# Relative attentions: unweighed probabilities are turned, and the inverse row sums are spread by a small matmul and multiplied in where the heads are copied

## The chip, the core and the metric

The kernel runs on one core of a Trainium2 chip. Its time is the device time of one execution in microseconds (us). Before the change it is 2825.42 us, the median of 3 runs (2820.93 to 2825.87).

The engines are named as in the profile: PE is TensorE (PEld its weight load, which overlaps the matmuls), DVE is VectorE, ACT is ScalarE, POOL is GpSimd, SP issues the DMAs (SPq is its queue).

## The reference, cut to what matters

The program is a chain of eight layers on a tensor of 4 x 512 tokens with 128 features. Two of them are attentions with 16 heads of 8 features, in which the distance of query and key also has its own learned key and value. The first is causal, the second sees all keys. Each head of each query has one row of 512 scores, and a softmax over it:

```python
# first relative attention (causal); rk, rv = embk[rel], embv[rel]
att = jnp.einsum('bhtd,bhsd->bhts', q, k) * scale + jnp.einsum('bhtd,tsd->bhts', q, rk)
att = jnp.where(causal[None, None], att, -jnp.inf)
att = jax.nn.softmax(att, axis=-1)
y = jnp.einsum('bhts,bhsd->bhtd', att, v) + jnp.einsum('bhts,tsd->bhtd', att, rv)
# second relative attention (all keys), same shape of work
attn = jax.nn.softmax((score1 + s2) / scaling, axis=-1)
w1 = jnp.einsum('bhqk,bhkd->bhqd', attn, vh)      # with the values v = h @ Wv.T + bv
w2 = jnp.einsum('qnk,qkd->qnd', se, rel_v)         # with the values of the distance
out = (w1 + w2) ...
```

A softmax row is exp(score - max) divided by its sum. Both products behind it are linear in the row, so the division may stand before them or behind them.

## The kernel before, in words

Each relative attention is one `core` step. It goes over 256 tiles. A tile is 8 queries by 16 heads of one lane (one of the 4 sequences): its 128 rows lie on the 128 partitions, and its columns are the keys, up to 512. 16 tiles are a batch (one block of 128 queries of a lane), so that there are 16 batches in each attention. All engines walk through the same steps `T_` = 0, 2, 4, ..., two tiles in each, and each stage handles the tile `T_ - lag`: scores at lag 6 (`SCORES`), turning at 8, the distance values at 10, their choice at 12. Each engine's code is written in the order in which it executes, and semaphores join the engines; there is no scheduler. The order within a step of two tiles is:

- PE: `scores` of two tiles (5 matmuls each of 128 rows in fp32r, one more in the causal attention), every other step `spread` (2 matmuls into bank 6), `turn` of the two tiles of the step before (up to 4 transposes each, L1033), `embedded` (small strip matmuls with the distance values), a part of `values` in steps 24, 26, 28 and 30 of a batch (mod 16: 8, 10, 12, 14), and `fold` at the steps in `FOLDS`.
- DVE: `chosen` twice (L1694), the copies of the position part (L1724, L1729, second attention only) and of the heads (L1745 in the first, L1747 in the second attention), `maxima` twice (L1709), then `normal` of the first tile (a reciprocal at L1686, a product over the whole row at L1687), every other step `diagonal` (L1702), and `normal` of the second tile.
- ACT: `exps` twice (L1364, with the row's sum as a second output), then the copies of the two turned tiles out of PSUM (by L1271).
- POOL: spreads queries with a mask (L1899, L1909) some steps ahead, and the values of a lane once per lane.

PE's `turn` waits for `r_normal`, the two rows weighed by DVE. PE's 4th matmul of the scores waits for `r_diagonal` when a new group of four tiles begins. `scores` of tile t + 2 waits for the exponentials of tile t, since there are two banks for scores. `values` accumulate a batch's heads in bank 7, and DVE copies them to `centered`.

## Time and profile before

| what | value |
|---|---|
| median of 3 runs | 2825.42 us (2820.93 to 2825.87) |
| the profiled execution | 2822.93 us, its span 2821.2 us |
| PE busy over the span | 2640.0 us (94%) |
| DVE, ACT, POOL busy | 1943.3, 1858.7, 1051.2 us |
| mean granted clock of TensorE | 0.977 of full speed |
| first relative attention, first to last matmul of its tiles | from about 616 to 1060 us |
| second relative attention | from about 1153 to 1719 us |

The profile shows one execution. "Busy" is the time in which an engine has an instruction in flight; for PE the ends of matmuls are modelled, and since matmuls overlap in the pipeline, their mean duration is longer than the distance from one to the next. That distance is read from the start times. A wait of PEld is partly covered by a matmul that still runs; a wait of PE itself is not covered, but begins only after the modelled end of the last matmul. The true stall lies between the two.

### The profile page before, as it was taken

How to read it: one execution, taken by the hardware profiler on the slowest of the kernel's cores; microseconds unless marked ns; L12 is line 12 of the kernel's file. 1: busy time of each engine (PE TensorE's matmuls, PEld its weight loads, DVE VectorE, ACT ScalarE, POOL GpSimd, SP SyncE). 2: the span in 40 equal slices, each digit the busy share in tenths (PEclk: the TensorE clock that was granted, in tenths of full speed). 3: DMA queues.
4: the chain of work that ended last, by engine and by line, in shares of the span. 5: the costliest groups of instructions: out<-in, count | busy, mean ns of one | idle time of the engine just before them, and what ended most of it. 6: DMA issues, size and time to landing. Idle time of an engine off the chain costs nothing.

```text
span 2821.2 us, 62773 instructions
## 1 busy us (share of the span) xinstructions
PE 2640.0 (94%) x23748; PEld 1795.2 (64%) x23748; DVE 1943.3 (69%) x5617; ACT 1858.7 (66%) x4392; POOL 1051.2 (37%) x876
## 2 busy tenths in 40 slices
PE   7999999899999998999999997999898997989998
PEld 5665657458888884688888884554455563553554
DVE  5564747488878777789898986774774326765774
ACT  5676767427676671678777875885776416866874
POOL 2322324113333320555555552552453014542551
PEclk9999999999999999999999999999999999999999
DMA  1010000000000001000000003210210002201210
GB/s 56 1 43 1 13 9 1 4 10 2 2 2 2 2 2 56 24 2 2 2 2 2 2 2 114 50 42 8 65 46 12 24 1 72 50 24 34 50 39 16
DMA packets 35278, 63.09 MB, mean 22 GB/s; under 512 B 11526, under 2 KB 15654, under 8 KB 33830
## 3 DMA queue, kind: packets, MB, share of 16 engines
q1 hardware_dynamic: 34982, 59.07, 7.6%
q8 instruction: 195, 3.19, 0.5%
q14 instruction: 101, 0.83, 0.1%
HBM read 23.48 MB, written 1.15 MB: 9 GB/s over the span
## 4 chain that ended last, share of the span: by engine, by line
PE 73%; DVE 12%; ACT 7%; issue 3%; SPq 2%; POOL 1%; DMA 1%; DVEq 0%; ACTq 0%; POOLq 0%
PE bank L804 63%; PE bank L1033 5%; PE bank L1153 3%; SPq L770 2%; PE bank L880 1%; ACT low L1364 1%; DVE low L1709 1%; DVE low L1687 1%; ACT work L1400 1%; ACT work L1303 1%; DVE halves L1702 1%; DMA work<-work 1%; DVE work L1589 1%; ACT bank L1279 1%; ACT squared L1281 1%
## 5 line engine op out<-in xcount | busy, mean ns | idle before, releaser
L1271 ACT ACTIVATE low<-bank 128x512 f32<-128x512 f32 (+3 forms) x512 | 427.7, 945 | 0.0
L804 PE MATMUL bank<-table_keys,halves 128*128 128x512 f32 (+3 forms) x1536 | 417.9, 380 | 1.2 <-ACT low L1364 1.0
L1364 ACT ACTIVATE low<-bank,low 128x512 f32<-128x512 f32 (+23 forms) x384 | 227.2, 592 | 248.9 <-DVE low L1709 244.9
L804 PE MATMUL bank<-work 128*64 128x128 f32 (+6 forms) x4192 | 344.9, 296 | 41.4 <-DVE work L1796 20.4
L804 PEld LDWEIGHTS bank<-work 128*64 128x64 f32 (+4 forms) x4192 | 249.7, 145 | 205.3 <-issue 151.7
L1709 DVE TENSOR_REDUCE low<-bank 128x1 f32<-128x512 f32 (+22 forms) x512 | 286.3, 569 | 94.5 <-PE bank L804 89.9
L1899 POOL TENSOR_TENSOR halves<-squared,const 128x512 fp32r<-128x512 f32 x128 | 136.9, 1070 | 510.9 <-PE bank L804 510.9
L1271 ACT ACTIVATE work<-bank 128x512 f32<-128x512 f32 (+4 forms) x389 | 199.8, 539 | 136.0 <-PE bank L804 70.2
L804 PEld LDWEIGHTS bank<-table_keys,halves 128*128 128x128 f32 x1536 | 243.6, 190 | 47.8 <-issue 13.3
L1400 ACT ACTIVATE work<-work 128x192 f32<-128x192 f32 (+1 forms) x512 | 218.8, 431 | 37.7 <-DVE work L1789 37.7
L1948 POOL TENSOR_TENSOR work<-work 128x768 f32<-128x768 f32 x128 | 187.7, 1466 | 136.0 <-DVE work L1800 136.0
L1953 POOL TENSOR_TENSOR work<-work 128x512 f32<-128x512 f32 x128 | 163.6, 1278 | 180.8 <-DMA work<-work 167.6
L1687 DVE TENSOR_SCALAR low<-low 128x512 f32<-128x512 f32 (+23 forms) x384 | 214.0, 557 | 13.5
L804 PE MATMUL bank<-halves 128*128 128x128 f32 (+27 forms) x1024 | 206.0, 283 | 11.5 <-DVE halves L1702 11.3
L804 PEld LDWEIGHTS bank<-halves 128*128 128x128 f32 x1024 | 181.5, 189 | 51.3 <-DVE halves L1702 23.9
L804 PE MATMUL bank<-normed,slot 128*128 128x512 f32 x440 | 198.8, 594 | 6.2 <-ACT work L1322 2.4
L804 PE MATMUL bank<-work,slot 128*128 128x512 f32 (+1 forms) x408 | 194.4, 614 | 5.6 <-ACT work L1271 5.6
L1275 ACT ACTIVATE squared<-centered 128x512 f32<-128x512 f32 x80 | 50.0, 629 | 222.1 <-DVE centered L1520 221.8
L1033 PE MATMUL bank<-const,low 128*128 128x128 f32 x1248 | 180.3, 274 | 5.0 <-ACT low L1271 3.9
L1857 POOL TENSOR_SCALAR normed<-normed,slot 128x512 f32<-128x512 f32 x48 | 75.4, 1571 | 286.8 <-DVE normed L1527 286.5
L804 PE MATMUL bank<-centered,const 128*128 128x512 f32 x256 | 145.0, 649 | 25.4 <-ACT centered L1377 25.4
L1942 POOL TENSOR_TENSOR work<-work 128x512 f32<-128x512 f32 (+1 forms) x64 | 107.5, 1680 | 150.7 <-DVE work L1603 149.5
(202 smaller groups left out, 5701.5 us busy)
## 6 DMA issues: line engine op xcount, KB each, us to landing
work<-work SPq DMA_DIRECT2D x512, 64.0 KB, 2.0
slot<-in_wW SPq DMA_DIRECT2D x4, 1605.5 KB, 7.0
slot<-in_wA SPq DMA_DIRECT2D x4, 837.0 KB, 6.2
table_low<-embv_padded SPq DMA_DIRECT2D x2, 1536.0 KB, 6.3
table<-in_dft SPq DMA_DIRECT2D x1, 3072.0 KB, 11.9
slot<-in_wE SPq DMA_DIRECT2D x2, 584.0 KB, 4.3
const<-in_const SPq DMA_DIRECT2D x1, 1094.5 KB, 5.3
squared<-in_x SPq DMA_DIRECT2D x4, 256.0 KB, 6.3
```

The lines of the kernel that those rows point to most:

```text
L804: return pe.matmul(o, l, r, start=start, stop=stop)
L1033: last = pe.transpose(o[:, b * P:(b + 1) * P], PR[t.G % 4][:, b * P:(b + 1) * P], ident)
L1153: last = pe.transpose(o[:, (2 * a + blk) * P:(2 * a + blk + 1) * P], PW[:, s.n % 3, 2 * u + a, blk * P:(blk + 1) * P], ident)
L1271: return act.activation(dst, src, ACT.Identity)
L1364: act.activation(PR[t.G % 4][:, 0:n], bank[t.G % 2][:, 0:n], ACT.Exp, bias=NBR[:, t.G % 4:t.G % 4 + 1], accum_out=RSR[:, t.G % 8:t.G % 8 + ...
L1400: last = act.activation(row, row, ACT.Exp, scale=-1.0, bias=small[:, one:one + 1], accum_out=small[:, 4 + one:5 + one])
L1687: dve.tensor_scalar(row, row, inverse, None, ALU.mult).then_inc(sem("r_normal"), 1)
L1709: dve.tensor_reduce(out=NBR[:, t.G % 4:t.G % 4 + 1], in_=bank[t.G % 2][:, 0:score_columns(t)], axis=AX.X, op=ALU.max, negate=True).then_in ...
L1899: pool.tensor_tensor(A4[:, half, Q % 2, :].rearrange("p (t h) -> p t h", h=HEADS_R), bc(one_lane.unsqueeze(2), [P, 4 * QG, HEADS_R]), bc(k ...
L1942: pool.tensor_tensor(row, row, bc(small_a[:, 8 + s.i % 4, 0:LOC].unsqueeze(2), [P, LOC, 256 - lo]), ALU.mult)\
L1948: pool.tensor_tensor(row, row, bc(small_w[:, s.n % 4, 8:12].unsqueeze(2), [P, 4, 192]), ALU.mult).then_inc(sem("w_weighed"), 1)
L1953: pool.tensor_tensor(R1[:, s.n % 3, :], R1[:, s.n % 3, :], R2[:, s.n % 3, :], ALU.add).then_inc(sem("w_added"), 1)
```

## The change

1. `normal` is gone on DVE (a reciprocal and a product over the row for each of 512 tiles). The exponentials stay unweighed: `turn` waits for `r_exp` instead of `r_normal`.
2. ACT's sums of a batch go to one array `RSR` of 16 columns (two of them in turns).
3. Once per batch, at step 22, DVE's `inverse` takes the reciprocal of 128 x 16 sums and multiplies it with a mask into `SPREAD_INVERSE` (128 x 128). PE's `inverse`, between `turn` and `embedded`, multiplies that with `head_rows` into columns 128 to 255 of bank 7, and in the second attention also with `swapped_rows` into the next 128. ACT's `inverse` copies the result to `INVERSE_SUMS` after the turned tiles. `values` of that batch (step 24) waits for that copy.
4. The copy of a batch's heads becomes a product with `INVERSE_SUMS` (first attention), and in the second a product and an addition instead of one instruction. The position copies become products. The value bias is added to two columns (`EVC`) before the second attention.
5. `FOLDS` of the second attention: the fold of a batch's first half moves from step 18 to step 24, its position copy from step 20 to 26.
6. The exact constants (568 columns) leave `const`, which becomes 1885 columns wide instead of 2189, and have a DMA of their own into `shifted`, ahead of the inputs on SP's queue.

```diff
-FOLDS, VALUES = ((24, 26), (18, 26)), 24
+FOLDS, VALUES, INVERSE = ((24, 26), (24, 26)), 24, 22
...
             sp.dma_start(const[:, :], ins["const"]).then_inc(sem("const_loaded"), 16)
+            sp.dma_start(exact_staged, ins["exact"]).then_inc(sem("exact_loaded"), 16)
...
                 def turn(t):
-                    pe.wait_ge(sem("r_normal"), t.at + 1)
+                    pe.wait_ge(sem("r_exp"), t.at + 1)
...
+                def inverse(T_):                                     # PE
+                    k = batch_after(T_, INVERSE)
+                    if k is None:
+                        return
+                    pe.wait_ge(sem("r_inverse_spread"), BATCHES * s.which + k + 1)
+                    reached(pe, "r_head_copied", BATCHES * s.which + k)
+                    last = mm(bank[7][:, P:2 * P], k_("head_rows"), SPREAD_INVERSE)
+                    if s.which:
+                        last = mm(bank[7][:, 2 * P:3 * P], k_("swapped_rows"), SPREAD_INVERSE)
+                    last.then_inc(sem("r_inverse"), 1)
...
                     if part == 0:
                         pe.wait_ge(sem("r_values_spread"), 4 * (C * s.which + lane) + 4)
-                        reached(pe, "r_head_copied", BATCHES * s.which + k)
+                        pe.wait_ge(sem("r_inverse_copied"), BATCHES * s.which + k + 1)
...
+                def inverse(T_):                                     # ACT, behind turned
...
+                    act.wait_ge(sem("r_inverse"), BATCHES * s.which + k + 1)
+                    reached(act, "r_head_copied", BATCHES * s.which + k)
+                    copy(INVERSE_SUMS[:, 0:1 + s.which, :], bank[7][:, P:(2 + s.which) * P].rearrange("p (a t) -> p a t", a=1 + s.which))\
+                        .then_inc(sem("r_inverse_copied"), 1)
...
+                        link(dve.tensor_tensor(EVC[:, 0:2], EVC[:, 0:2], bc(wt(s, WR, "bv"), [P, 2]), ALU.add))
...
-                def normal(t):
-                    inverse = RIR[:, t.G % 8:t.G % 8 + 1]
-                    row = PR[t.G % 4][:, 0:score_columns(t)]
-                    dve.wait_ge(sem("r_exp"), t.at + 1)
-                    link(dve.reciprocal(inverse, RSR[:, t.G % 8:t.G % 8 + 1]))
-                    dve.tensor_scalar(row, row, inverse, None, ALU.mult).then_inc(sem("r_normal"), 1)
+                def inverse(T_):                                     # DVE
...
+                    dve.wait_ge(sem("r_exp"), s.which * TILES + BATCH * (k + 1))
+                    reached(dve, "r_inverse", BATCHES * s.which + k)
+                    link(dve.reciprocal(RIR, RSR[:, k % 2, :]))
+                    wide = [P, BATCH, QG]
+                    dve.tensor_tensor(SPREAD_INVERSE.rearrange("p (t q) -> p t q", q=QG), bc(RIR.unsqueeze(2), wide),
+                                      bc(k_("row_query").unsqueeze(1), wide), ALU.mult).then_inc(sem("r_inverse_spread"), 1)
...
-                            copied = dve.tensor_copy(PH[rows_, one, :], bank[6][32 * one:32 * one + 32, 0:64])
+                            dve.tensor_tensor(PH[rows_, one, :], bank[6][own, 0:64], INVERSE_SUMS[own, 1, 64 * half:64 * half + 64], ALU.mult)\
...
-                            last = dve.tensor_copy(dst, o)
+                            last = dve.tensor_tensor(dst, o, weigh, ALU.mult)
...
-                            last = dve.scalar_tensor_tensor(out=dst, in0=o, scalar=wt(s, WR, "bv"), in1=dst, op0=ALU.add, op1=ALU.add)
+                            link(dve.tensor_tensor(weighed, o, weigh, ALU.mult))
+                            last = dve.tensor_tensor(dst, dst, weighed, ALU.add)
...
                     position_copy(T_)
                     head_copy(T_)
+                    inverse(T_)
                     st(maxima, SCORES)
                     st(maxima, SCORES - 1)
-                    st(normal, SCORES)
                     st(diagonal, SCORES - 2)
-                    st(normal, SCORES - 1)
```

How the instructions stand now is shown at three places. Names in them: `slot` and `low` hold DVE's results and the rows of probabilities, `halves` the spread queries, `table_keys` the keys, `bank` is PSUM; the semaphores in brackets are what a row waits for.

DVE in the second attention, steps 36 and 38 (20 and 22 of the second batch), before: the position copy, the maxima, the weighing of two rows with `diagonal` between, and the next two maxima.

```order
L1724 COPY low<-bank 32x64 [waits r_folded]
L1724 COPY low<-bank 32x64 x3
L1729 SCALAR_TENSOR_TENSOR centered<-low,centered 32x4x64 [waits r_position_copied]
L1709 TENSOR_REDUCE low<-bank 128x1 [waits r_scores,r_position_added]
L1709 TENSOR_REDUCE low<-bank 128x1 [waits r_scores]
L1686 RECIPROCAL low<-low 128x1 [waits r_exp]
L1687 TENSOR_SCALAR low<-low 128x512 [waits vector_chain]
L1702 TENSOR_TENSOR halves<-bank,const 128x512 [waits r_repeated]
L1686 RECIPROCAL low<-low 128x1 [waits r_exp]
L1687 TENSOR_SCALAR slot<-slot,low 128x512 [waits vector_chain]
L1694 TENSOR_TENSOR slot<-bank,const 128x16x8 [waits r_embedded] x2
L1709 TENSOR_REDUCE low<-bank 128x1 [waits r_scores] x2
```

The same steps now:

```order
L1724 TENSOR_TENSOR slot<-bank,const 128x16x8 [waits r_folded,r_embedded]
L1724 TENSOR_TENSOR slot<-bank,const 128x16x8 [waits r_embedded]
L1739 TENSOR_REDUCE low<-bank 128x1 [waits r_scores] x2
L1732 TENSOR_TENSOR halves<-bank,const 128x512 [waits r_repeated]
L1724 TENSOR_TENSOR slot<-bank,const 128x16x8 [waits r_embedded] x2
L1714 RECIPROCAL low<-low 128x16 [waits r_inverse,r_exp]
L1716 TENSOR_TENSOR low<-low,const 128x128 [waits vector_chain]
L1739 TENSOR_REDUCE low<-bank 128x1 [waits r_scores] x2
```

The `diagonal` (L1732 now) follows the maxima at once, without a wait for an exponential; the position copy has left this step; the two rows of `inverse` stand ahead of the maxima of step 38.

PE in step 38 of the second attention, before: the end of the scores, the turning, the distance values.

```order
L804 MATMUL bank<-halves 128x376 [waits r_diagonal]
L804 MATMUL bank<-halves 128x376
L1033 MATMUL bank<-const,low 128x128 [waits r_turn_copied,r_normal]
L1033 MATMUL bank<-const,low 128x128 x3
L1033 MATMUL bank<-const,slot 128x128 [waits r_turn_copied,r_normal]
L1033 MATMUL bank<-const,slot 128x128 x3
L804 MATMUL bank<-low,shifted 32x16x4 [waits r_chosen,r_turn_copied]
```

And now:

```order
L807 MATMUL bank<-halves 128x376 [waits r_diagonal]
L807 MATMUL bank<-halves 128x376
L1036 MATMUL bank<-const,low 128x128 [waits r_turn_copied,r_exp]
L1036 MATMUL bank<-const,low 128x128 x3
L1036 MATMUL bank<-const,slot 128x128 [waits r_turn_copied,r_exp]
L1036 MATMUL bank<-const,slot 128x128 x3
L807 MATMUL bank<-low,const 128x128 [waits r_head_copied,r_inverse_spread]
L807 MATMUL bank<-low,const 128x128
L807 MATMUL bank<-low,shifted 32x16x4 [waits r_chosen,r_turn_copied]
```

The turning waits for the exponentials alone, and the two small matmuls stand between full-width work and the strips, where the array changes its tiling anyway.

PE at step 34 (18 of the second batch) before, where the fold stood directly ahead of the next scores:

```order
L804 MATMUL bank<-low,table_low 32x16x4 x2
L804 MATMUL bank<-slot,const 32x64 [waits r_position_copied,r_diagonal,r_chosen]
L804 MATMUL bank<-slot,const 32x64 x15
L804 MATMUL bank<-table_keys,halves 128x512 [waits r_exp]
L804 MATMUL bank<-table_keys,halves 128x512 x2
```

And now, at step 40 (24):

```order
L807 MATMUL bank<-low 32x128 [waits r_inverse_copied,r_values_spread]
L807 MATMUL bank<-low 32x128 x15
L807 MATMUL bank<-slot,const 32x64 [waits r_position_copied,r_diagonal,r_chosen]
L807 MATMUL bank<-slot,const 32x64 x15
L807 MATMUL bank<-table_keys,halves 128x512 [waits r_exp]
```

The fold (the 16 rows of 32x64) stands behind a part of the values now, in a step that is longer, and the first values wait for the copy of the inverse sums.

## Rows read from the trace of the kernel before

**Rows 1.** Windows: PE, PEld, DVE, ACT, POOL busy; clock, DMA share, GB/s.
```profile
1200.00:1300.00 100.00, 99.07 (x1475) 83.33 (x1475) 86.13 (x229) 78.37 (x137) 51.94 (x45) 1.00 0.01 2
```
**Rows 2.** Waits of PE, PEld, 611 to 1052 us: total us, times, longest.
```profile
PE bank L804 <- DVE halves L1702: 6.2, 15, 0.8
PEld bank L804 <- DVE halves L1702: 11.6, 27, 1.0
PEld bank L804 <- ACT low L1364: 1.9, 9, 0.3
```
**Rows 3.** The same waits, 1149 to 1716 us.
```profile
PE bank L804 <- DVE halves L1702: 5.1, 16, 0.5
PEld bank L804 <- DVE halves L1702: 12.3, 17, 0.9
PEld bank L804 <- ACT low L1364: 2.5, 9, 1.0
```
**Rows 4.** Timeline, steps 38 and 40 of the second attention: start, us, engine, what.
```profile
1223.59 0.81 DVE L1687 TENSOR_SCALAR low<-low 128x512 f32<-128x512 f32 x1
1223.80 0.97 PE L804 MATMUL bank<-table_keys,halves 128*128 128x512 f32 x3
1224.08 1.31 POOL L1909 TENSOR_TENSOR halves<-squared,const 128x512 fp32r<-128x512 f32 x1
1224.32 0.68 DVE L1702 TENSOR_TENSOR halves<-bank,const 128x512 fp32r<-128x512 f32 x1
1225.05 0.30 PEld L804 LDWEIGHTS bank<-halves 128*128 128x128 f32 x2 [0.72 <-DVE halves L1702]
1225.36 1.32 POOL L1909 TENSOR_TENSOR halves<-inner,const 128x512 fp32r<-128x512 f32 x1
1225.51 0.86 PE L804 MATMUL bank<-table_keys,halves 128*128 128x512 f32 x3
1226.00 1.45 DVE L1709 TENSOR_REDUCE low<-bank 128x1 f32<-128x512 f32 x2
1227.52 0.32 PE L804 MATMUL bank<-low,shifted 128*32 128x64 f32 x8
1228.09 0.96 PE L804 MATMUL bank<-table_keys,halves 128*128 128x512 f32 x3
1228.15 2.01 ACT L1271 ACTIVATE low<-bank 128x512 f32<-128x512 f32 x2
1229.23 0.86 PE L804 MATMUL bank<-table_keys,halves 128*128 128x512 f32 x3
1232.16 1.04 PE L804 MATMUL bank<-low 128*32 128x128 f32 x30
```
**Rows 5.** Timeline, start of the second attention.
```profile
1158.74 2.93 DVE L1687 TENSOR_SCALAR low<-low 128x512 f32<-128x512 f32 x1
1160.48 0.67 PE L804 MATMUL bank<-halves,exact 128*128 128x512 f32 x2
1164.33 0.97 PE L804 MATMUL bank<-table_keys,halves 128*128 128x512 f32 x3 [0.75 <-ACT low L1364]
```
**Rows 6.** Line L1687: ns min/median/max, first and last start, forms.
```profile
L1687 DVE TENSOR_SCALAR low<-low x384: 244/487/2930, 619.9 to 1708.9; 128x512 f32<-128x512 f32 x104, 128x128 f32<-128x128 f32 x8, 128x256 f32<-128x256 f32 x8, 128x384 f32<-128x384 f32 x8
```
**Rows 7.** Timeline: 8 records of full fp32 matmuls, and 8 transposes.
```profile
606.19 1.05 PE L804 MATMUL bank<-slot,normed 128*128 128x128 f32 x8
...
1204.42 1.04 PE L1033 MATMUL bank<-const,low 128*128 128x128 f32 x8
```
**Rows 8.** Groups by form, 1149 to 1723 us: busy us, mean ns, idle before.
```profile
L1724 DVE COPY low<-bank 32x64 f32<-32x64 f32 x128 | 28.2, 220 | 7.8 <-PE bank L804 4.3
```
**Rows 9.** The page, part 6: KB, us from issue to landing.
```profile
const<-in_const SPq DMA_DIRECT2D x1, 1094.5 KB, 5.3
```
**Rows 10.** Timeline: last turned tiles and values of the second attention.
```profile
1709.26 3.80 ACT L1271 ACTIVATE low<-bank 128x512 f32<-128x512 f32 x4
1713.33 2.84 PE L804 MATMUL bank<-low 128*32 128x128 f32 x64
```

More of the change, by code:

```diff
@@ L1371, in core @@
                     st(turned, TURN - 1)
+                    inverse(T_)
             def w_rotate(s):
@@ L1722, in position_copy @@
                         rows_ = slice(32 * lane, 32 * lane + 32)
+                        dve.wait_ge(sem("r_inverse_copied"), BATCHES + k + 1)
+                        dve.wait_ge(sem("r_head_copied"), BATCHES + sum(VALUES + QG + BATCH * one < T_ for one in range(BATCHES)))
                         for one in range(C):
[L1724 to L1725 removed]
+                            own = slice(32 * one, 32 * one + 32)
+                            dve.tensor_tensor(PH[rows_, one, :], bank[6][own, 0:64], INVERSE_SUMS[own, 1, 64 * half:64 * half + 64], ALU.mult)\
+                                .then_inc(sem("r_position_copied"), 1)
                         dve.wait_ge(sem("r_position_copied"), 4 * folds_before(1, T_))
@@ L1972, in shape_constants @@
     p = np.arange(P)
-    const = np.zeros((P, CONST_W), np.float32)
+    const, exact = np.zeros((P, CONST_W), np.float32), np.zeros((P, EXACT_W), np.float32)
     def put(name, a):
-        at, w = CONST[name]
-        const[:a.shape[0], at:at + w] = a
+        whole, (at, w) = (const, CONST[name]) if name in CONST else (exact, EXACT[name])
+        whole[:a.shape[0], at:at + w] = a
     put("ident", np.eye(P))
@@ L1982, in shape_constants @@
     put("pair_ones", p[:, None] // D_W == p[None, :] // D_W)
+    row = p[:, None] % HEADS_R
+    put("head_rows", row == p[None, :] // D_R)
+    put("swapped_rows", row == C * (p[None, :] % 32 // D_R) + p[None, :] // 32)
+    put("row_query", p[:, None] // HEADS_R == np.arange(QG)[None, :])
     put("low_rows", np.where(p[:, None] % 32 < DH_A, 0.0, -1.0))
@@ L2024, in shape_constants @@
     dft = np.concatenate([forward.reshape(P, -1), inverse.reshape(P, -1)], 1).astype(np.float32)
-    return {"const": const, "rotary": rotary, "dft": dft}
+    return {"const": const, "exact": exact, "rotary": rotary, "dft": dft}
 def lay_out(inputs):
```

35 lines of the change are left out of this document (23 added, 12 removed).

## The prediction, made before the changed kernel ran

> **What bounds the kernel now.** I read the windows first. In a stretch of either relative attention PE is busy nearly all the time, 99.07 of 100 us in the second, at full clock, while DVE stands at 86.13 and ACT at 78.37 [rows 1]. So work taken from DVE is worth nothing by itself: only the pauses that PE makes for DVE can come back, and each matmul that is added there is paid in full. The two attentions cover about 1010 us of the span, and the change touches little else.
>
> Then I asked for the waits of PE and of its weight loads. The largest with a named releaser is PE's 4th matmul of the scores waiting for `diagonal` (L1702). PE itself idled 6.2 us for it in the first attention and 5.1 in the second, its weight loads 11.6 and 12.3 [rows 2, 3]. Waits of the weight loads for exponentials (L1364) add 1.9 and 2.5 us. These two columns bracket the true stall: a load's wait is partly covered by the matmul in front, and a matmul's wait counts only from that matmul's modelled end.
>
> The timeline settles where between the two it lies. In step 38 the scores of one tile start at 1223.80 and those of the next at 1225.51, 1.71 us later, with the wait in between; in step 40 the same distance is 1228.09 to 1229.23, 1.14 us, without one [rows 4]. The shapes differ by 16 columns, which is nothing. The stall is 0.57 us where the load's wait is 0.72, so 0.78 of the load's wait is real.
>
> The same rows show why `diagonal` is late. It stands behind the weighing of a row (L1687), which itself waits for an exponential and here took 0.81 us against a median of 0.487 [rows 6]: POOL was spreading queries at that time and started its next instruction at 1224.08, and DVE was done only after that. Once, at 1158.74, the same instruction took 2.93 us [rows 5]. The trace shows this slow form only for the row product and only beside POOL.
>
> That is what the Trainium skill says in "SBUF — State Buffer", section "Who interferes with whom": a VectorE `tensor_scalar` in a two-port mode and a GpSimd instruction lock each other out for a whole instruction. The trace agrees, with 2.93 us against 0.487. The rule also speaks against the change, since a `tensor_tensor` with both inputs in SBUF, as the new mask product, is said to meet the same lock; that is a rival below.
>
> **The change part by part.** The working is against the profiled execution, 2822.93 us with its span of 2821.2; it lies within the three runs, 2.5 us under their median.
>
> 1. *Waits for `diagonal` go.* 11.6 + 12.3 = 23.9 us of waits of the loads, times 0.78, is 18.6 us. `diagonal` now comes directly behind the two maxima, so it is earlier by one wait for an exponential, a reciprocal and a row product. In step 38 DVE was free for it by 1223.59, when the row product started instead; it would have ended by 1224.27, and PE wanted it at about 1225.05 - 0.57 = 1224.5 [rows 4]. What is late next: in the shortest steps (one block of keys, first attention) the spread matmuls, two maxima and the 0.68 us of L1702 itself nearly fill the step, and the very first group has no row product ahead of it and stalls as before. I leave 1.5 us standing. The gain's bounds are 6.2 + 5.1 = 11.3 us (PE's own waits alone) and 23.9. I take 17.1.
>
> 2. *The start of the second attention.* PE finished a spread pair begun at 1160.48 and could take the next scores only at 1164.33 [rows 5]. Unhindered, from the spread to the next scores it is the pair (about 0.5 us), 8 transposes of 0.109 (0.9 us) and a change of tiling: about 1.6 us instead of 3.85. The maxima and exponentials of that step are then also early, as the row product of 2.93 us is gone. Gain 2.0, bounds 0.75 (the wait named there) and 2.3.
>
> 3. *Waits for exponentials.* 1.9 + 2.5 us of loads' waits, 1.0 of it in the start just counted: 3.4 x 0.78 = 2.7 us. The maxima start sooner once DVE has less to do, so half goes: 1.3, bounds 0 and 2.7.
>
> 4. *Added matmuls.* 16 batches with one and 16 with two: 48 matmuls of 128x128 in fp32 with 128 columns. In [rows 7] 8 records of such matmuls take 1.05 us, of which the last lasts 0.275: one every 0.111 us. Four matmuls make these 8 records (the value projection), so a matmul is 0.222 us, and 48 are **10.7 us**, all on PE's path. Lower bound: they run like the transposes beside them, one record of 0.109 each, 5.2 us. Upper bound: both records cost their whole 0.275, as they do at the end of a dependent group, 26.4 us; nothing waits directly behind them except ACT, so I stay at the nearest row. They stand between transposes and strips and add no change of tiling. The moved fold costs PE the same at its new place.
>
> 5. *Added waits.* DVE's `inverse` has what it needs from the step before; PE wants it some 3 us into the step. ACT's copy stands behind the two turned copies. In step 38 those end at 1228.15 + 2.01 = 1230.16 and the values start about 1232.1 [rows 4]; the new copy has 256 columns, a quarter of those two together, so about 0.5 us. Slack 1.4 us, so the 32 waits cost 0; behind the values' wait stand the fold and the next scores, so a late copy would be paid in full. At the tail no scores come between: the last turned copies end at 1713.06, the values began at 1713.33 [rows 10]; with the copy they begin at about 1713.6. With the same in the first attention: +0.3, bounds 0 and 0.8. ACT itself is 0.5 us busier once in 8 steps, covered by its idle share.
>
> 6. *Copies of heads and position.* Products instead of copies, the same size and one PSUM operand; in the second attention one instruction more (0.25 to 0.5 us by the range of L1687's forms, [rows 6]) once per batch on an engine that has lost two row products per step. Only the last one is on the path: +0.3. The two additions to the bias columns before the second attention: +0.2. The move of the fold takes the position copy (4 of 0.220 us, [rows 8]) out of the last scoring step, which lets the last maxima start earlier: -0.9. Together -0.4, bounds -1.2 and +1.
>
> 7. *The start.* Ahead of the inputs stand 304 columns less in `const` and 568 more in a DMA of their own: 264 columns, 132 KB more. By const's 1094.5 KB in 5.3 us [rows 9] that is at most 0.64 us, and SP issues one more DMA, hidden under const's transfer: +0.5, bounds 0 and 1.
>
> 8. *Work that DVE loses* (512 reciprocals, 512 products) beyond these stalls: 0. PE's own work hides it.
>
> Sum: -17.1 - 2.0 - 1.3 + 10.7 + 0.3 - 0.4 + 0.5 = **-9.3 us**, so 2813.6 from the profiled execution. I predict **2814 us**.
>
> **The rivals.**
>
> *Same, because only PE's own waits return.* If what the load's column names is covered by running matmuls, then -11.3 - 0.75 + 10.7 + 0.4 = -1.0, or 2822. For it: PE shows 99% busy. Against: the distance of starts in [rows 4].
>
> *Same, because the bunched position work stalls PE.* Both folds of a batch now come two steps apart, with four copies and an addition on DVE behind each, over 1 us [rows 8], and the spread of step 28 waits for the second. A stall of 0.5 us in each of 16 batches gives back 8 us: 2821.6. For it: one such stall per batch is there today. Against: today it falls in a step without values; steps 26 and 28 have 1 us more of PE work (the 30 records in 1.04 us of [rows 4]), and the spread comes 2 us into the step.
>
> *Better.* The matmuls cost one pass (5.2 instead of 10.7) and all of the loads' waits return: -23.9 - 2.3 - 2.7 + 5.2 + 0.4 = -23 at the far end, about -16 (2807) when only one of both holds.
>
> *Slower, by the mask product.* Its inputs, the reciprocals and `row_query`, both lie in SBUF, and in step 22 of a batch POOL runs two spreads back to back, 1224.08 to 1226.68. If DVE is held until both are done, its two maxima start at about 1227.0 instead of 1226.00, the exponentials follow, and the scores of the next step (1228.09) wait for them. That decides from the point where the maxima start later than about 1226.4. Price: some 0.8 us in each of 32 batches, 26 us: 2840. For it: the 2.93 us in [rows 5], longer than any one POOL instruction. Against: that happened once in 512, while the common delay (0.81) ends with the POOL instruction in progress; a mask product released at 1225.4 is early enough. By the skill's rule the product may be held for the instruction that runs, at most 1.32 us, which gives no more than the forecast.
>
> **How the numbers follow.** Forecast 0.62, held waits "PE's own" 0.12, bunched position work 0.09, better 0.10, slower 0.07. What a measurement of this kernel can tell from no change is about 0.2%, 5.7 us. The forecast and "better" are beyond it: faster 0.72; the two "same" cases 0.21; slower 0.07. The forecast's own range is 2809 to 2819. For 8 in 10 it reaches into "better" down to 2806 and over both "same" cases to 2823.
>
> **What would show it.** In the profile after: no L1687; the weight loads' wait for `diagonal` (L1732) under 3 us in both attentions together; `bank<-low,const` full-width matmuls as 96 records of about 0.11 us distance; DVE near 60 of 100 us in a window of the second attention with PE still near 99%; no wait of PE for ACT's inverse copies except at the two ends; and the mask product (L1716) not over 1.6 us. It would be wrong if the distance from one batch to the next in the second attention fell by less than 0.2 us or grew: that says that the matmuls cost more than the stalls, or that a new wait took their place.

## The result: 2799.5 us, about twice the gain forecast, and the profile after

The changed kernel takes 2799.5 us (median of four runs, 2798.1 to 2801.4). The kernel before, run beside it, takes 2823.2. The ratio is 0.9928, 95% interval 0.9906 to 0.9949. A second set of runs gave 0.9938 (0.9921 to 0.9954), so the gain is 20 us by the first ratio and 17 by the second, and the two intervals together span 13 to 27. The 23.7 us between the first two medians flatter the change: beside the later sets the kernel before took 2817.8 to 2820.4. The forecast was 9.3 and its wider range ended at 2806: the sign was right and the size wrong.

The profiled execution took 2798.09 us, span 2796.1. The window that answers to [rows 1] (PE, PEld, DVE, ACT, POOL busy; clock, DMA share, GB/s):

```profile
1200.00:1300.00 100.00, 100.00 (x1496) 85.66 (x1495) 63.46 (x149) 80.16 (x143) 49.87 (x51) 1.00 0.01 2
```

DVE fell from 86.13 to 63.46 us and PE has no pause left in this window. The waits of PE and its weight loads in the first attention (607 to 1040 us), to be held against [rows 2]:

```profile
PE bank L807 <- DVE halves L1732: 0.8, 2, 0.5
PEld bank L807 <- ACT low L1379: 1.9, 9, 0.3
PEld bank L807 <- DVE halves L1732: 1.1, 2, 0.6
```

In the second attention no wait for `diagonal` (now L1732) over 0.2 us is left, where [rows 3] had 12.3. The added work, first in the timeline (four records of inverse sums' matmuls in 0.61 us, then ScalarE's two turned copies with the inverses' copy as a third), then the mask product by its line (ns min/median/max):

```profile
1209.75 0.61 PE L807 MATMUL bank<-low,const 128*128 128x128 f32 x4
1210.48 2.22 ACT L1286 ACTIVATE low<-bank 128x512 f32<-128x512 f32 x3
```

```profile
L1716 DVE TENSOR_TENSOR low<-low,const x32: 291/474/1085, 633.2 to 1687.3; 128x128 f32<-128x128 f32 x32
```

I used one more measure throughout: the time from the first tile's first scores matmul to the last tile's ("the scores stretch" below), in each attention, and the same from the first tile to the 17th for the first batch of the second attention. It repeats within about 0.4 us between executions of one kernel, while whole executions scatter by 10 us and more.

| kernel | median, us | ratio to before (95%) | attention 1 | attention 2 | its first batch |
|---|---|---|---|---|---|
| before | 2823.18 | 1 | 431.1 | 551.2 | 33.9 |
| changed | 2799.51 | 0.9928 (0.9906, 0.9949) | 422.9 | 541.5 | 28.6 |
| after_again | 2800.86 | 0.9938 (0.9921, 0.9954) | 422.9 | 541.1 | 28.2 |
| before_again | 2822.25 | 1.0011 (0.9999, 1.0023) | 431.1 | 551.4 | 34.0 |
| exact_dma | 2817.69 | 1.0000 (0.9988, 1.0013) | 430.9 | 551.3 | 34.0 |
| diag_first | 2838.09 | 1.0070 (1.0053, 1.0087) | 430.8 | 569.7 | 34.1 |
| before_folds (24) | 2811.45 | 0.9978 (0.9966, 0.9989) | 431.1 | 543.8 | 33.3 |
| before_folds20 | 2819.61 | 1.0000 (0.9986, 1.0013) | 431.1 | 556.6 | 36.2 |
| before_folds22 | 2813.61 | 0.9984 (0.9972, 0.9995) | 431.1 | 547.1 | 34.1 |
| before_memset | 2816.12 | 0.9989 (0.9977, 1.0001) | 431.1 | 549.3 | 32.0 |
| before_tt | 2856.97 | 1.0135 (1.0113, 1.0157) | 440.7 | 576.1 | 34.6 |
| double | 2808.78 | 0.9961 (0.9947, 0.9975) | 426.4 | 548.1 | 28.5 |
| no_matmul | 2792.74 | 0.9906 (0.9892, 0.9920) | 420.2 | 534.7 | 28.5 |
| ones_folds18 | 2794.06 | 0.9908 (0.9890, 0.9925) | 420.2 | 534.8 | 28.7 |
| product_back | 2818.78 | 0.9995 (0.9982, 1.0009) | 430.0 | 551.4 | 33.3 |
| product_short | 2808.98 | 0.9971 (0.9956, 0.9987) | 428.1 | 547.6 | 34.7 |
| reduce_short | 2803.04 | 0.9949 (0.9931, 0.9966) | 423.3 | 542.2 | 28.6 |
| reduce_part | 2799.67 | 0.9935 (0.9918, 0.9951) | 423.3 | 542.2 | 28.6 |
| recip_back | 2819.61 | 1.0002 (0.9987, 1.0017) | 432.2 | 551.4 | 33.3 |
| one_pass | 2789.43 | 0.9899 (0.9881, 0.9917) | 420.8 | 537.2 | 28.5 |

The two attentions gave 8.3 + 9.7 = 18.0 us. The other 7 us between the two profiles lie outside them, in code that the change leaves alone. The windows of the two stretches, before and then changed, show how long PE itself idled in them (the length less PE's busy time, the first two numbers):

```profile
617.30:1048.50 431.20, 424.61 (x6394) 366.37 (x6393) 349.50 (x1096) 297.63 (x760) 136.65 (x136) 1.00 0.01 2
1154.40:1705.60 551.20, 543.60 (x7835) 454.73 (x7833) 478.77 (x1246) 430.50 (x760) 297.17 (x264) 0.99 0.01 2
```

```profile
613.50:1036.40 422.90, 421.92 (x6424) 369.53 (x6422) 229.22 (x618) 300.45 (x775) 133.72 (x136) 1.00 0.01 2
1142.80:1684.30 541.50, 541.50 (x7863) 462.89 (x7861) 341.88 (x788) 434.37 (x774) 274.65 (x264) 1.00 0.01 2
```

That is 6.6 + 7.6 = 14.2 us before and 1.0 in the changed kernel.

### The profile page after: what moved, and what is told of

It is laid out like the page before. It is cut to its first block, busy times and chain, and to the rows that moved or that the text cites. A ratio compares the mean times of both kernels' runs of the same rounds, so it can differ in the third digit from the quotient of the medians.

```text
span 2796.1 us, 62201 instructions
## 1 busy us (share of the span) xinstructions
PE 2630.2 (94%) x23844; PEld 1800.8 (64%) x23844; DVE 1681.3 (60%) x4679; ACT 1866.1 (67%) x4424; POOL 1025.4 (37%) x876
## 3 DMA queue, kind: packets, MB, share of 16 engines
HBM read 23.62 MB, written 1.15 MB: 9 GB/s over the span
## 4 chain that ended last, share of the span: by engine, by line
PE 78%; DVE 8%; ACT 6%; issue 3%; SPq 3%; POOL 1%; DMA 1%; DVEq 0%; POOLq 0%; ACTq 0%
PE bank L807 67%; PE bank L1036 6%; PE bank L1168 3%; SPq L772 3%; ACT work L1425 1%; ACT work L1318 1%; PE bank L883 1%; DVE work L1614 1%; ACT bank L1294 1%; ACT squared L1296 1%; ACT squared L1290 1%; POOL work L1984 1%; DMA work<-work 1%; ACT work L1286 1%; DVE centered L1545 0%
## 5 line engine op out<-in xcount | busy, mean ns | idle before, releaser
L807 PE MATMUL bank<-work 128*64 128x128 f32 (+6 forms) x4192 | 343.3, 294 | 40.1 <-DVE work L1832 20.4
L1724 DVE TENSOR_TENSOR slot<-bank,const 128x128 f32<-128x128 f32 x512 | 126.6, 287 | 102.7 <-PE bank L807 101.9
## 6 DMA issues: line engine op xcount, KB each, us to landing
table<-in_dft SPq DMA_DIRECT2D x1, 3072.0 KB, 11.8
```

What stands on the lines that cost most here:

```text
L807: return pe.matmul(o, l, r, start=start, stop=stop)
L1724: dve.tensor_tensor(WB[:, half, :, t.cols], bank[4 + t.G % 2][:, 0:P].rearrange("p (h q) -> p h q", h=HEADS_R), k_("own_query").rearrange( ...
```

## The experiments

### Is the rest the change's own?

**before_again** is the kernel before; **after_again** the changed one. No edit.

> The kernel before, once more. By the theory that the clock is what differs outside the attentions (its half-clock stretches fall elsewhere in each execution), the part up to the first scores (617.3 us in the first profile of it, 613.5 with the change) or the part behind the second attention (1102.2 and 1099.1) comes out 2 us or more from the first profile, while both attentions together stay within 2 us of 431.1 and 551.2. By the rival (what lies outside is fixed by the program, and the change itself gave 7 us there), both parts come out within 0.5 us of 617.3 and 1102.2.

> The changed kernel once more, beside the runs of the kernel before. If the 7 us outside the attentions were one execution's, the ratio to before comes out near the 18 us of the attentions alone (0.9935) and the profile's parts outside the attentions differ by 2 us or more from those of the first profile (613.5 us up to the first scores). If they are the change's own, the ratio stays at 0.991 to 0.993 and the parts come out the same within 0.5 us.

Both attentions came out the same within 0.4 us. The part up to the first scores took 617.3 and 617.7 us in the two profiles of before; among the kernels built on before it went from 612.0 to 617.7, among those built on the changed one from 612.6 to 618.3. The part behind the second attention's last scores varies more, 1115.5 and 1117.9 in before, 1111.8 and 1123.4 in the changed kernel. So the 7 us were those two executions' own. By the outer part before_again spoke for its second theory and after_again for the first; only all profiles together settle it.

**exact_dma**: before, with the constants' load as in the change.

```
-  ("repeat", 192), ("causal_query", 128), ("causal_rows", 248)     in const
+  sp.dma_start(exact_staged, ins["exact"])                         a load of its own
```

> Only the load of the constants as in the change: three blocks leave the first load and come by one of their own. By the forecast +0.5 us (a longer start, the first matmul 0.4 us later) and nothing elsewhere. By the rival that the 7 us outside the attentions belong to this part of the change (a smaller first load, another layout), -4 to -7 us, with the part up to the first scores near 613.5.

Ratio 1.0000, first matmul 0.13 us later here and 0.41 in the changed kernel: the load is worth nothing.

### What do the added matmuls cost?

**double** makes each inverse sums' matmul twice:

```
-  last = mm(bank[7][:, P:2 * P], k_("head_rows"), SPREAD_INVERSE)
+  for _ in range(2):
+      last = mm(bank[7][:, P:2 * P], k_("head_rows"), SPREAD_INVERSE)
```

> The changed kernel with each matmul of the inverse sums made twice, 48 more of them. By the forecast's price (0.222 us each, all on PE's path) +10.7 us: +3.6 in the first attention, +7.1 in the second, 0.44 a batch in the latter. By the rival that they partly fill pauses of PE, so that the error of the forecast was this price, under +5 us.

**no_matmul** drops them, their waits and ScalarE's copy, so that the rows are not divided:

```
-  inverse(T_)                      PE and ScalarE
+  link(dve.memset(INVERSE_SUMS, 1.0))
```

> The changed kernel without the 48 matmuls of the inverse sums and without ScalarE's copy of them: the heads are multiplied by ones in place of the inverse sums, so the rows aren't divided; the product that spreads the inverses on DVE, the heads' multiplications and everything else stay. By the forecast -10.7 us (-3.6 and -7.1); -11 to -13 if the waits around them (PE for the spread, the copies for ScalarE) cost something too. By the rival price under -5 us.

48 more cost 3.5 + 6.6 = 10.1 us, 48 fewer save 2.7 + 6.8 = 9.5. The price of 10.7 was right within about 1 us, and the error isn't there. **one_pass** makes them in the short format:

```
-  mm(bank[7][:, P:2 * P], k_("head_rows"), SPREAD_INVERSE)         fp32
+  mm(bank[7][:, P:2 * P], exact_("head_rows"), SPREAD_INVERSE)     fp32r, both
```

> The changed kernel with the inverse sums' matmuls made in one pass (the spread inverses and the two masks rounded to the short format that the scores' keys have) in place of full precision. The 48 matmuls took 0.2 us each by the runs with twice as many and with none; the turns' scores in the short format take a quarter of the time for a column, so 0.06 each: -7 us (-2.5 in the first attention, -4.7 in the second), or -2 to -4 if a small matmul costs mostly its weight load.

It saves 2.1 + 4.2 = 6.3 us in the attentions and is the fastest of all kernels here, 1.0% under before.

### Was it the order on DVE?

**diag_first** exchanges two lines of the kernel before:

```
-  st(normal, SCORES)
   st(diagonal, SCORES - 2)
+  st(normal, SCORES)
   st(normal, SCORES - 1)
```

> The kernel before with one exchange on DVE: the diagonal mask product is put ahead of the first row product (and of its wait for the exponential), nothing is taken out. By the theory that PE waited for `diagonal` because it stood in the row behind the wait for an exponential, most of what the change took away goes here too: -12 to -18 us, PE's waits for L1709 down from 23.9 us to under 5. By the rival that DVE was simply too full in those steps (length, not order), -1 to -5 us, and the waits stay above 12 us or move to the turns, which then get their rows later.

The waits for `diagonal` went (these are the waits that the expectation puts down to L1709; their line is L1702) and nothing was gained: the first attention took 0.3 us less, the second lost 18.5. The same views as [rows 2 and 3], weight loads' waits, of diag_first, first 605 to 1052 us, then 1149 to 1716:

```profile
PEld bank L804 <- ACT low L1364: 11.4, 29, 0.7
PEld bank L1033 <- DVE slot L1687: 2.4, 5, 1.5
...
PEld bank L804 <- ACT low L1364: 20.3, 37, 1.0
PEld bank L1033 <- DVE slot L1687: 5.7, 16, 0.4
```

A wait of 11.6 us for one name came back as 11.4 for another. The name at the end of a wait says who came last, not who was too slow: exponentials are late when the maxima are (ScalarE waited 99.5 us for the maxima between 1200 and 1690 us of before, and 122.1 between 1200 and 1700 of diag_first), and the maxima of a step stand behind the row products of the step before. That the products made them late is argued here, not shown, and why the second attention lost so much stays open. My theory that moving `diagonal` forward brings the gain fell here.

### Was it the row product?

**product_back** is the changed kernel with a product (by 1.0, without the reciprocal) in its old place and nothing else undone:

```
+  dve.wait_ge(sem("r_exp"), t.at + 1)
+  dve.tensor_scalar(row, row, 1.0, None, ALU.mult).then_inc(sem("r_normal"), 1)
-  pe.wait_ge(sem("r_exp"), t.at + 1)            ahead of the turn
+  pe.wait_ge(sem("r_normal"), t.at + 1)
```

> The changed kernel with only the row product put back on DVE in its old place (a multiplication of each row by 1.0 that waits for the exponential, and PE's turn waits for it); everything else of the change stays. If the row product is what the first attention's 11.8 us and the rest of the second's came from, and the move of the fold from step 18 to 24 the other 7.4: +11 to +13 in the first attention, +9 to +10 in the second, +20 to +23 in all, and the start of the second attention back at about 33 us. By the forecast's sizes +20.4 in all with 2.0 at the start of the second attention. If the move of the fold and the product hide behind each other, the second attention gives back less than 6.

It gives back 7.1 and 10.0 us, and with it the slow start (33.3). In the first attention I had expected 11 to 13. These 17.1 us are nearly the net gain of 18.0, but the kernel still has the added matmuls: of the 28 to 29 us that came back before the matmuls took their share, 11 were not the product's. **product_short** multiplies only 8 columns:

```
-  row = PR[t.G % 4][:, 0:n]
+  row = PR[t.G % 4][:, 0:8]
```

> As the one with the row product put back, but the product covers only the row's first 8 columns: the two handshakes (DVE for the exponential, PE's turn for DVE) and the order stay, the length goes. If the order and the handshakes made the 17 us that the whole product cost (7.1 in the first attention, 10.0 in the second): +13 to +17 against the changed kernel. If the length of the product on a full DVE made them: +0 to +4, first attention near 423 to 425 us, second near 541 to 544, and the second attention's start at 28.5 to 29.5 us in place of 33.3.

8 columns still cost 5.2 and 6.1 us, 11.3 of the 17.1, which is less than the theory of order (13 at least) and more than the theory of length (4 at most) allowed; the other 5.8 come with the length. The start is worse than ever (34.7). Its timeline there (start, us, engine, what) shows why:

```profile
1153.20 1.13 POOL L1953 TENSOR_TENSOR halves<-inner,const 128x512 fp32r<-128x512 f32 x1
1153.24 7.04 DVE L1723 TENSOR_SCALAR low<-low 128x8 f32<-128x8 f32 x2
...
1154.28 1.80 POOL L1980 MEMSET centered<- 128x2048 f32 x1
1154.35 5.94 DVE L1745 TENSOR_REDUCE low<-bank 128x1 f32<-128x512 f32 x2
...
1158.07 1.11 POOL L1953 TENSOR_TENSOR halves<-squared,const 128x512 fp32r<-128x512 f32 x1
1159.14 1.11 POOL L1953 TENSOR_TENSOR halves<-inner,const 128x512 fp32r<-128x512 f32 x1
1160.33 1.87 PE L1036 MATMUL bank<-const,low 128*128 128x128 f32 x8 [4.49 <-DVE low L1723]
```

Its line (ns min/median/max, 1149 to 1200 us):

```profile
L1723 DVE TENSOR_SCALAR low<-low x17: 159/172/7033, 1153.2 to 1196.6; 128x8 f32<-128x8 f32 x17
```

The first multiplication of 8 columns took 7.03 us where 0.16 is its least, the maxima queued in DVE behind it end with it, and all end at 1160.28, when GpSimd's unbroken run ends at 1160.25. PE stood 4.49 us.

One place proves little, so I counted all products of a trace by whether a GpSimd instruction ran during them. In product_short the 265 that met none took 0.155 to 0.175 us, the 247 others 0.171 to 7.03, on average 0.60. In the second attention of before, where all rows have 512 columns, the 120 that met none took 0.485 to 0.491 us, the 136 others up to 2.93, on average 0.68. Only products beside GpSimd were ever late.

**reduce_short** and **reduce_part** keep the waits, the order and, the latter, the length in time, and change the form:

```
-  dve.tensor_scalar(row, row, 1.0, None, ALU.mult)
+  dve.tensor_reduce(out=scrap[...], in_=row, axis=AX.X, op=ALU.max)   row: 8 columns, or n * 5 // 8
```

> As product_short (the changed kernel with a short operation of 8 columns put back on DVE between the exponential and the turn, both handshakes kept), but the operation is a maximum over the 8 columns written elsewhere, not a multiplication in place. If the form of the multiplication made the cost (it waits for a pause of GpSimd): the start of the second attention back at 28.2 to 28.8 us (34.7 with the multiplication), and the first attention near 423 to 424 us (428.1). If the order and handshakes made it: 34 us and 428 us again.

> As reduce_short with a maximum over five eighths of the row, as long as the row product took alone (0.4 us), so that order, handshakes and length are as in the kernel with the product back, and only the form differs. If the form is what counts: the second attention's start at 28.3 to 29.5 us (33.3 with the product), the first attention at 424 to 427 (430.0). If length and order count: 430 and 551 us again.

Both cost 0.4 and 0.8 us where the multiplication of the same 8 columns cost 5.2 and 6.1. The same place of reduce_part:

```profile
1146.04 1.13 POOL L1954 TENSOR_TENSOR halves<-inner,const 128x512 fp32r<-128x512 f32 x1
1146.10 0.48 DVE L1724 TENSOR_REDUCE scrap<-low 128x1 f32<-128x320 f32 x1
...
1147.03 0.49 DVE L1724 TENSOR_REDUCE scrap<-low 128x1 f32<-128x320 f32 x1 [0.45 <-ACT low L1380]
...
1147.11 1.81 POOL L1981 MEMSET centered<- 128x2048 f32 x1
1147.43 1.50 DVE L1746 TENSOR_REDUCE low<-bank 128x1 f32<-128x512 f32 x2
...
1148.55 1.04 PE L1037 MATMUL bank<-const,low 128*128 128x128 f32 x8
...
1149.34 0.95 PE L808 MATMUL bank<-table_keys,halves 128*128 128x512 f32 x3
```

GpSimd runs as densely, the reductions take 0.48 and 0.49 us beside it, and PE doesn't stop. This is the experiment that settles it: the cost was the product's form, and place, waits and length cost 1.2 us without it. The length counts only in that form. Two things stay open: the reduction also writes a single column where the product writes its row, and these runs don't part that from the operation; and no run takes GpSimd's work away, so its share rests on the timelines, on the count above and on the next run.

**before_memset** moves GpSimd's clearing of the heads:

```
-  if s.which and T_ == BATCH // 2:
+  if s.which and T_ == BATCH - 4:
```

> The kernel before with GpSimd's clearing of the heads (1.8 us) at step 12 of the second attention in place of step 8. If it is this clearing beside which one of the first row products takes 2.93 us, the start of the second attention loses PE's 2.5 us of idling and the half-clock stretch behind it: the first batch 33.9 us to 29 to 31, -3 to -5 in all. If GpSimd's spreads alone hold the product up, or the stall only moves to the products at the new place, within 1 us of before, first batch 33 to 34.5.

The product that took 2.93 us in [rows 5] took 1.19, and the first batch became 1.9 us shorter, less than the theory's 3 to 5: the clearing was a part of the unbroken run, and at its new place a product beside it took 1.38.

**before_tt** changes the form in the kernel before, which I expected to give the whole gain (a product of two tensors in place of one with a scalar):

```
-  dve.tensor_scalar(row, row, inverse, None, ALU.mult)
+  dve.tensor_tensor(row, row, bc(inverse, [P, score_columns(t)]), ALU.mult)
```

> The kernel before with one instruction in another form: the row product is a product of two tensors (the row and its inverse sum, repeated along the row) in place of a product with a scalar. By the theory that the scalar form waits for GpSimd and this one doesn't: first attention 420 to 424 us in place of 431.1 (423.3 with order and length kept and 3.5 us of matmuls, and the reciprocals' 2), second 535 to 543 in place of 551.2, -14 to -22 in all, as much as the whole change gave, with no stall at the second attention's start. By the rival that a product of two tensors in SBUF is slowed by GpSimd's reads as much (or is so much longer, 0.6 us for 0.5, that DVE becomes full): 0 to -6.

It lost 9.6 and 24.9 us. This form takes 0.69 us at best in the second attention (its line, 1160 to 1690 us), and GpSimd's spreads beside it 1.52 us (groups, 1180 to 1680 us: busy us, mean ns, idle before) where the kernel before has 1.26 and reduce_part 1.15:

```profile
L1687 DVE TENSOR_TENSOR low<-low x175: 691/692/1601, 1163.3 to 1689.6; 128x512 f32<-128x512 f32 x175
```

```profile
L1909 POOL TENSOR_TENSOR halves<-inner,const 128x512 fp32r<-128x512 f32 x55 | 83.5, 1519 | 0.0
```

So both the longer form and the collision count, and this run doesn't part them.

**recip_back** adds the reciprocals to product_back:

```
+  link(dve.reciprocal(RIR[:, t.g:t.g + 1], RSR[:, t.batch % 2, t.g:t.g + 1]))
   dve.tensor_scalar(row, row, 1.0, None, ALU.mult)
```

> The row product put back, and ahead of each the reciprocal of its sum and the wait for it, as in the kernel before. The kernel before spent 431.1 us in the first attention's scores, the one with the product alone 430.0 with 3.5 us of added matmuls in it, so 4.7 us of the first attention are left to the 256 reciprocals: then 434 to 435 us there; in the second, where 0 is left to them by the same sum, 551 to 552. By the rival that the 4.7 us came of something else in the change (the copies of the heads, the next batch's buffers), under 1 us more than the product alone: 430 to 431.

2.3 us in the first attention, half of what I expected, 0 in the second. Of the first attention's 11.8 us (8.3, and 3.5 for the matmuls by double), 7.1 are the product's, 2.3 the reciprocals', and 2.4 stay without a run. The old product took its factor from a column, and was longer by it (0.49 us at least on 512 columns, 0.42 with the constant); that this is the 2.4 was not tried.

### Was it the move of the fold?

**before_folds**, **before_folds20** and **before_folds22** are the kernel before with the second attention's first fold at step 24, 20 and 22:

```
-  FOLDS, VALUES = ((24, 26), (18, 26)), 24
+  FOLDS, VALUES = ((24, 26), (24, 26)), 24        (20, 26) and (22, 26) in the others
```

> The kernel before with the folds of the second attention at steps 24 and 26 in place of 18 and 26, as the change has them, and all else as before. If the place of the first fold and of its position copy is worth something (the copies stood ahead of a PE wait of 0.15 to 0.29 us a batch), -1 to -4 us, all of it in the second attention. By the forecast, which priced it within the copies at nothing, within 1 us of before. By the rival that four more copies in the crowded step 28 hurt, +1 to +3.

> The kernel before with the second attention's first fold at step 20 in place of 18; its position copies come two steps later, at 22 in place of 20. If what counts is that the four copies and the addition don't share a step with DVE's mask product (steps 20, 24, 28 have one, 22 and 26 don't): -6 to -8 us in the second attention (551.2 to 543.5 to 545), as with the fold at 24 and the copies at 26. If the distance counts (a later fold, a value of its own for each step): a third of it, -2 to -3.

> The kernel before with that fold at step 22, its position copies at step 24, in one step with a mask product again. If the shared step counts: within 1.5 us of before in the second attention (550 to 552.5). If the distance counts: -4 to -6 (545 to 547).

The move to 24 alone gave 7.4 us, more than any of my three expectations, to 22 it gave 4.1, and to 20 it cost 5.4 in the second attention. My theory of a step shared with `diagonal`, the mask product of that expectation, is wrong: 20 should have been as good as 24. The theory of distance is no better, since 20 should have given something. Why one step is better than another stays open. At 24 the weight loads' wait for `diagonal`, 12.3 us in [rows 3], is down (before_folds, 1149 to 1716 us):

```profile
PEld bank L804 <- DVE halves L1702: 3.6, 4, 1.0
```

**ones_folds18** asks what the move is worth without row products:

```
   (no_matmul)
-  FOLDS, VALUES, INVERSE = ((24, 26), (24, 26)), 24, 22
+  FOLDS, VALUES, INVERSE = ((24, 26), (18, 26)), 24, 22
```

> The changed kernel without the inverse sums' matmuls (the heads are multiplied by ones, so the rows aren't divided), with the second attention's first fold back at step 18 and its position copies at 20. Its neighbour with the fold at 24 took 534.7 us in the second attention. If the place of the fold mattered only because a full DVE stood in scalar products that wait for GpSimd: within 1.5 us of that, 533 to 536. If it matters by itself (the copies and the mask product in one step): +4 to +8, 539 to 543.

534.8 against 534.7 us: nothing. So the move is worth something only while the row products are there, and what each is worth depends on which goes first: from before, the move gives 7.4 and the rest of the change 2.3 more (9.4 with the matmuls' 7.1 set off); in the kernel without row products the move gives 0. By this run, which leaves the added matmuls out, item 5 of the change was not needed.

## Why the prediction was wrong

**The step that failed is the size of the terms 1 to 3, the stalls that go.** They summed to 17.1 + 2.0 + 1.3 = 20.4 us. The attentions gave 18.0 and paid for the matmuls 3.6 + 7.1 = 10.7, or 10.1 by double: 28 to 29 us of stalls went. By place (scores stretch, the matmuls added back at double's price): the first attention, about 9 forecast and 11.8 measured; the second behind its first batch, about 9 and 11.0; the start, 2.0 and 5.3 (its first batch ends ahead of the first added matmuls: double has 28.5 us there, the changed kernel 28.6). By cause: the product 17.1 (product_back), the reciprocals 2.3, the move of the fold, with products present, about 7, and 2.4 open. PE's own idle time fell by 13.2 us only; about half of what came back had never shown as a pause of PE (the ends of its matmuls are modelled), and even all of the loads' waits that carry the name `diagonal`, 23.9 us, are less than what came back.

- *Term 1, the waits for `diagonal`.* The mechanism was half right. These waits went (1.3 us of loads' waits left), but they were taken as the price and as the cause. I put the delay down to the product's place ahead of `diagonal`; diag_first shows that putting `diagonal` first gains nothing, and reduce_part that the same place and length with another form costs 1.2 us in all. I had the cause in hand, the 0.81 us against 0.487 beside GpSimd and the 2.93, and used it only to explain one wait. The 0.78 from one step was then applied to one name's column, though the same delays also reach PE where no wait carries that name. In product_back those loads' waits are 6.1 us in the first attention, where the product costs 7.1, and 1.2 in the second, where it costs 10.0.
- *Term 2, the start.* The gaps were seen and what followed them in this execution was missed: the granted clock fell again behind them. Windows of before, then of the changed kernel, then of diag_first (last columns: clock, DMA share, GB/s):

```profile
1158.00:1165.00 7.00, 5.04 (x23) 3.42 (x23) 6.65 (x9) 2.28 (x7) 7.00 (x7) 0.94 0.01 4
1165.70:1169.00 3.30, 3.20 (x12) 2.92 (x13) 2.10 (x6) 1.88 (x5) 0.44 (x1) 0.50 0.00 0
```

```profile
1150.00:1160.00 10.00, 10.00 (x92) 8.39 (x91) 5.97 (x12) 9.77 (x18) 8.23 (x8) 1.00 0.00 1
```

```profile
1155.00:1162.00 7.00, 5.05 (x24) 3.54 (x22) 6.40 (x8) 2.00 (x7) 7.00 (x7) 0.89 0.01 4
1162.00:1166.00 4.00, 3.82 (x36) 2.98 (x37) 3.65 (x9) 3.69 (x7) 1.85 (x2) 1.00 0.00 0
```

  PE idled 2.0 us in the first window of before, and then ran 3.3 us at 0.50 (1.2 GHz), which is up to 1.65 us lost; the changed kernel has neither this pause nor this fall. (Both kernels run the first microseconds of the attention at 0.50, behind the gap between the attentions.) product_short repeats it: 0.52 for 3.5 us behind its pause. But diag_first idled as long in its first window, 1.95 us, and kept its clock at 1.00 after, so the fall doesn't follow every such pause; before idled another 0.5 us just behind its first window, where the clock fell. The first batch of before idled 2.5 us in all; with the 1.65 that makes 4.1 of the 5.3 us, and the rest is not accounted for.
- *Term 3, exponentials.* In the first attention the loads' wait for them stayed 1.9 us; in the second nothing of it is left. Half, as forecast.
- *Term 4, the matmuls.* 10.7 forecast; 10.1 and 9.5 by two runs. Right; the rival "better" had put them at 5.2.
- *Terms 5 and 6.* No wait for the inverse copies inside the attentions. The tails gave 0.2 and 0.6 us. "The moved fold costs PE the same" holds without row products (ones_folds18), but in the kernel before the move alone gave 7.4 us, where this term had -0.9 for it.
- *Term 7.* 0.41 us at the first matmul, 0.5 forecast; exact_dma, with the same load, has 0.13.
- *Term 8, "work that DVE loses: 0".* By length, right: reduce_part puts 0.33 and 0.48 us a row back and costs 1.2 us. But the reciprocals alone cost 2.3 in the first attention (recip_back), and the work is not free without limit, as before_tt shows.
- *The rivals.* "PE's own waits only" is refuted: they would have brought 12 us, and 28 came. The bunched position work and the mask product stall nothing that shows (no wait of PE names them inside the attentions). The mask product was held at times: 1.085 us at most where the 9 of 32 that met no GpSimd instruction took 0.295 at most. "Better", at 23 us less, came nearer to the time than the forecast, for reasons that didn't hold: cheap matmuls and no more than the named waits. That is luck. And every sign that I had named for the forecast came true (waits for `diagonal` of 1.3 us, DVE at 63.46, PE at 100, the mask product at 1.085): they tested that the waits go, not how much that is worth.

The Trainium skill says in "SBUF — State Buffer", section "Who interferes with whom", that `tensor_scalar` in a two-port mode and GpSimd exclude each other, that a `tensor_tensor` with two inputs in SBUF meets GpSimd's reads, and that `tensor_reduce` on this chip never does. All three agree here: up to 7.03 us for 8 columns, spreads of 1.52 us beside before_tt's products, and reductions of 0.489 us at most in reduce_part. I cited it for its danger to the change, one product in eight steps, and not for what it said of the instruction that went, which ran 512 times. One point differs: that section has the loser wait for the other's instruction; here in the longest case it waited for the one in progress and five more.

## What to carry to other kernels

When an instruction on a busy engine goes, look at the stretch of the instruction itself (its mean against its least, and what runs on the neighbour at that time), not only at the wait that ends at the bounding engine. The stretch tells the cause and not the price: the products of product_back's second attention that ran beside GpSimd took about 45 us more than unhindered ones (137 of 0.753 us against 0.426), and cost 10.0. Here a short operation of the wrong form cost two thirds of a long one. To learn whether order, length or form is at fault, keep the handshakes and exchange the operation for one of equal length that the traces never show late. And a gain measured for one part of a change says little about that part beside the others: here the same move was worth 7.4 us or nothing.

## What the runs showed of the hardware

- A DVE multiplication by a scalar, SBUF to SBUF in fp32, can starve behind GpSimd: once 8 columns took 7.03 us, until GpSimd's back-to-back instructions paused, and what DVE had queued behind it ended with it. The full row at the same place (product_back) was done after 3.11 us, while GpSimd ran on. None of the 265 that met no GpSimd instruction took over 0.175 us.
- A reduction from the same rows was never delayed: 0.489 us at most in all 512 of them, beside GpSimd (251) or not.
- Pauses of PE early in the second attention, 2.5 us together in before and 4.5 in product_short, were followed by over 3 us at half clock; 1.95 us of them in diag_first were not.
